# A graph network on one core: count products packed per group of eight nodes through three PSUM banks, and one PSUM bank for the attention sums

## The chip, the cores and the metric

The kernel runs on one core of a Trainium2 chip. Its time is the device time of one execution in microseconds (us), launch to end, as the median of several executions. A profiled execution gives one trace with the start and duration of each instruction on each engine: TensorE (PE, with its weight loads PEld), VectorE (DVE), ScalarE (ACT), GpSimd (POOL), SyncE (SP), whose queue (SPq) issues DMAs.

## What is computed

A graph of 6,250 nodes with 256 features and 100,000 edges sorted by destination. Two residual blocks:

```python
edge_index = jnp.stack([src, dst])
h = jnp.maximum(_layernorm(x, axis=-1), 0.0)
x = x + attention(h, edge_attr_16, edge_attr_4, W_n, attn_l, attn_r, attn_m, src, dst)
h = jnp.maximum(_layernorm(x, axis=-1), 0.0)
x = x + three_sage_layers(h, edge_index, ...)

# attention: 8 heads of 32 columns
e = leaky_relu((left[src] + right[dst] + edge part) / 3)    # per edge and head
a = softmax of e over the edges of one destination
out[dst] = sum over its edges of a * (feat @ W_n)[src]

# one SAGE layer
msg  = relu(x @ pW + pb)[src]
mean = segment_sum(msg, dst) / max(degree, 1)
out  = mean @ lW + lb + x @ rW, divided by its norm
```

## The kernel before, in words

Nodes are held in 49 blocks of 128, edges in 784 tiles of 128; seven tiles make a chunk, so there are 112 chunks. The kernel has three stages: preparation (projections into a table of rows), attention over the chunks, and the three SAGE layers. The change lies in the attention stage.

**The attention loop.** Every engine runs its own loop over steps `c` with the chunks taken at fixed offsets, in an order written out by hand; semaphores tie the engines. `Count.done(n)` is the value that the n-th signal of a semaphore makes, `free(n)` the value that says a buffer is free again; the number beside a name in `ATTENDED` is how many buffers are free at the start.

- GpSimd gathers the 896 source rows of a chunk with seven indirect DMAs into a ring of `RING = 7` chunks (`gather_chunk`, L621). The gather of chunk c waits for `summed(c - 7)`.
- TensorE, step c: a front part for the scores (`kinds_of`, `kind_tiles`, `to_heads`, `to_edges`, `left_of`; L1824 to L1862), then the sums of chunk c-1 (`sum_tiles`): for each of seven tiles a product of a one-hot matrix with the weighed rows (L1874, 128x265, float32, so two instructions each), accumulated in one PSUM bank, and one more product that adds what the chunk before left in the same window of nodes, moved by `shift_mat` (L1882). Its end is the signal `summed(c - 1)`. After it, in some steps, the projection of a finished block of nodes (`project`, L1930) or its transposition (`turn`, L1892).
- VectorE, step c: `below_max(c-1)` (L1999), `score_of(c+2)`, `run_maxima(c)` (ends with L1991), `weigh(c-1)` (L2014, the long product of rows and weights), the marks (below), then pieces of the work for a finished block of nodes (`biased`, `node_norm`, `node`) in 7 of 16 steps each, and `shifting(c)`.
- ScalarE, step c: `soften(c-1)` (L2166, L2167), `own_side(c)` (the one-hot matrices of the sums: seven times L2187, then L2191), `keep(c-2)` (L2197: sums from PSUM to SBUF), `other_side(c+4)` (L2175, L2178), and `turned`, `normed`, `positive` for a block of nodes.
- SyncE loads the edges of later chunks and stores the sums that `keep` has copied.

**The counts.** Beside the attention, in the 96 steps from 8 to 103, the stage builds a dense matrix of edge counts for the first 3,072 nodes, which the layers read later. Its 384 groups of eight nodes (`WIN = 8`) are taken in pairs, 192 duos, two duos to a step. For a duo q: VectorE writes marks (`mark`, eight compares, L2085 and L2086) into one of `MARKS = 3` buffers; TensorE forms the counts (`cross`, L1921: two accumulated float16 products for each of the two groups, 128x392 each, into banks 3 and 4); ScalarE packs both banks into bytes in one instruction (`pack`, L2221, 128x784). After 16 groups a stripe of 128 columns is complete and a DMA on ScalarE's queue stores it. `cross(q)` waits for `packed(q - 1)`, since there is one pair of banks.

**The order around the counts.** TensorE, step c: front part, `cross` of the first duo, four tiles of the sums (`HELD = 4`), `cross` of the second duo, three tiles and the shift. ScalarE, step c: `soften(c-1)`, `pack` of the first duo of step c-1, `own_side(c)`, `pack` of the second duo of step c-1, `keep(c-2)`, `turned`, `other_side(c+4)`, `normed`, `positive`. `own_side(c)` waits for `summed(c - 2)`, because it overwrites the one-hot matrices that those sums read. The sums of even and odd chunks lie in PSUM banks 6 and 7. In PSUM, bank 0 holds the scores, 1 the transposed scores, 2 the weights, 5 the block of nodes.

Of the kernel before, what the change touches and what calls it, by code (L numbers as in the profile page):

```python
# [35 lines left out]
ACT = mybir.ActivationFunctionType  # L36
# [7 lines left out]
TILES = 7  # L44
CHUNK = TILES * P
CHUNKS = -(-E // CHUNK)
# [1 line left out]
RING = 7  # L48
EDGES = 6
ENDS = 2  # L50
HELD = 4
assert CHUNKS % SLOTS == 0
TABLE = BLOCKS * P + P
FALL = 128
# [37 lines left out]
WIN = 8  # L92
WINS = DENSE // WIN
CROSS = BLOCKS * WIN
# [9 lines left out]
STRIPE = P  # L104
# [3 lines left out]
MARKS = 3  # L108
# [522 lines left out]
    return list(range(DUOS * (c - CROSS_FROM) // steps, DUOS * (c + 1 - CROSS_FROM) // steps))  # L631


def first_duo(c):

    return duos_at(c)[:1]


def later_duos(c):

    return duos_at(c)[1:]


def buffer_of(stripe):
# [569 lines left out]
def layers(nc, m, a, block, s, stored):  # L1214
# [461 lines left out]
ATTENDED = dict(  # L1676
    rows0=None, rows1=None, rows2=None, rows3=None, rows4=None, rows5=None, rows6=None, ends0=None, ends1=None, edges0=None,
    edges1=None, edges2=None, edges3=None, edges4=None, edges5=None, distance=0, oht=0, right=1, kinds=1, masked=0,
    scored=0, leaky=0, xt=1, bwd=0, mt=1, diff=1, expd=2, denoms=0, weighed=0, apart=0, onehot=0, shifted=0, summed=2, kept=2,
    store0=None, store1=None, sums=None, recips=0, norm=0, x1=0, stats=0, mv=0, newton=0, inv_norm=0, shift=0,  # L1680
    h=0, x1_put=None, htrans=0, ht=0, proj=0, evac=0, relu=0, put=None, runs=None, sorting=0, picked=0, taken=0, marked=0, crossed=0, packed=0, built0=None, built1=None)

# [1 line left out]
def attention(nc, m, a, block, s):  # L1684
# [132 lines left out]
    def _(pe):  # L1817
# [46 lines left out]
        def sum_tiles(c, tiles):  # L1864
            if not 0 <= c < CHUNKS:
                return
            parity, k = c % 2, c % RING
            if tiles[0] == 0:
                pe.wait_ge(s["denoms"].sem, s["denoms"].done(c))
                pe.wait_ge(s["weighed"].sem, s["weighed"].done(c))  # L1870
                pe.wait_ge(s["onehot"].sem, s["onehot"].done(c))
                pe.wait_ge(s["kept"].sem, s["kept"].free(c))
            for t in tiles:
                last = nc.tensor.matmul(m.ps[:, 6 + parity, 0:SUMC], m.one_hot[:, parity, t, :], m.ring[:, k, t, 0:SUMC],  # L1874
                                        start=(t == 0), stop=(c == 0 and t == TILES - 1))
            if tiles[-1] < TILES - 1:
                return
            if c:

                pe.wait_ge(s["kept"].sem, s["kept"].done(c - 1))  # L1880
                pe.wait_ge(s["shifted"].sem, s["shifted"].done(c - 1))
                last = nc.tensor.matmul(m.ps[:, 6 + parity, 0:SUMC], m.shift_mat[:, parity, :], m.sums_out[:, 1 - parity, :],  # L1882
                                        start=False, stop=True)
            last.then_inc(s["summed"].sem, 1)

# [22 lines left out]
                                        start=(j == 0), stop=(j == SORTS - 1))  # L1908
            last.then_inc(s["picked"].sem, 1)

        def cross(q):


            pe.wait_ge(s["marked"].sem, s["marked"].done(q))
            if q:
                pe.wait_ge(s["packed"].sem, s["packed"].done(q - 1))
            else:
                pe.wait_ge(s["taken"].sem, s["taken"].done(3))
            for i in range(2):
                for r in range(2):  # L1920
                    last = nc.tensor.matmul(m.ps[:, 3 + i, 0:CROSS], m.lane_marks[:, q % MARKS, 2 * i + r, :], m.cell_marks[:, q % MARKS, 2 * i + r, :],  # L1921
                                            start=(r == 0), stop=(r == 1))
            last.then_inc(s["crossed"].sem, 1)

        def project(n):
# [8 lines left out]
        for c in range(-4, steps):  # L1934
            if 0 <= c + 3 < CHUNKS:
                kinds_of(c + 3)
            kind_tiles(c + 3, range(0, TILES))
            if 0 <= c + 1 < CHUNKS:
                to_heads(c + 1)
            if 0 <= c < CHUNKS:  # L1940
                to_edges(c)
            if 0 <= c + 3 < CHUNKS:
                left_of(c + 3)
            for q in first_duo(c):
                cross(q)
            sum_tiles(c - 1, range(0, HELD))
            for q in later_duos(c):
                cross(q)
            sum_tiles(c - 1, range(HELD, TILES))
            if SORT_FROM < c <= SORT_FROM + 4:  # L1950
                pick(c - SORT_FROM - 1)
            for n in at_step(c, 3):
                project(n)
            for n in at_step(c, 2):
                turn(n)

    @block.vector
    def _(dve):
# [118 lines left out]
        def mark(q):  # L2077


            if q >= MARKS:  # L2080
                dve.wait_ge(s["crossed"].sem, s["crossed"].done(q - MARKS))
            for i in range(2):
                for r in range(2):
                    w = 2 * q + i
                    nc.vector.tensor_scalar(m.cell_marks[:, q % MARKS, 2 * i + r, :], m.cell_row, m.cell_at[:, r, w:w + 1], None, ALU.is_equal)  # L2085
                    last = nc.vector.tensor_scalar(m.lane_marks[:, q % MARKS, 2 * i + r, :], m.cell_row[:, 0:P], m.lane_of[:, r, w:w + 1],  # L2086
                                                   None, ALU.is_equal)
            last.then_inc(s["marked"].sem, 1)

        def node(n):  # L2090

# [68 lines left out]
    def _(act):  # L2160
# [32 lines left out]
        def keep(c):  # L2193
            act.wait_ge(s["summed"].sem, s["summed"].done(c))
            if c >= 2:
                act.wait_ge(s[f"store{c % 2}"], 16 * (c // 2))
            nc.scalar.activation(m.sums_out[:, c % 2, :], m.ps[:, 6 + c % 2, 0:SUMC], ACT.Copy).then_inc(s["kept"].sem, 1)  # L2197

        def normed(n):
            act.wait_ge(s["shift"].sem, s["shift"].done(n))  # L2200
# [8 lines left out]
                act.wait_ge(s["proj"].sem, s["proj"].done(n - 1))  # L2209
            nc.scalar.activation(m.b_hT[:], m.turned_h, ACT.Copy).then_inc(s["ht"].sem, 1)  # L2210

        def pack(q):


            stripe, place = divmod(q, STRIPE_DUOS)
            buffer = buffer_of(stripe)
            act.wait_ge(s["crossed"].sem, s["crossed"].done(q))
            if place == 0 and stores_before(stripe, buffer):
                act.wait_ge(s[f"built{buffer}"], 16 * stores_before(stripe, buffer))
            out = m.stripes[:, buffer, :].rearrange("p (b n) -> p b n", n=STRIPE)[:, :, 2 * WIN * place:2 * WIN * (place + 1)]  # L2220
            nc.scalar.activation(out.rearrange("p b (i n) -> p i b n", i=2), m.ps[:, 3:5, 0:CROSS].rearrange("p i (b n) -> p i b n", n=WIN),  # L2221
                                 ACT.Copy).then_inc(s["packed"].sem, 1)
            if place == STRIPE_DUOS - 1:
                act.wait_ge(s["packed"].sem, s["packed"].done(q))
                act.dma_start(m.adj[stripe], m.stripes[:, buffer, :]).then_inc(s[f"built{buffer}"], 16)

        def positive(n):
# [3 lines left out]
        for c in range(-4, steps):  # L2231
            if 0 <= c - 1 < CHUNKS:
                soften(c - 1)
            for q in first_duo(c - 1):
                pack(q)
            if 0 <= c < CHUNKS:
                own_side(c)
            for q in later_duos(c - 1):
                pack(q)
            if 0 <= c - 2 < CHUNKS:  # L2240
                keep(c - 2)
            for n in at_step(c, 3):
                turned(n)
            if 0 <= c + 4 < CHUNKS:
                other_side(c + 4)
            for n in at_step(c, 1):
                normed(n)
            for n in at_step(c, 4):
                positive(n)
# [454 lines left out]
```

## Time and profile before

| | |
|---|---|
| time, median of 3 executions | 3049.98 us (3046.11 to 3052.17) |
| the profiled execution | 3053.74 us, its span 3052.0 us |
| mean granted TensorE clock in it | 0.943 |
| busy over the span: PE / PEld / DVE / ACT / POOL | 87% / 61% / 73% / 54% / 66% |
| DMA | mean 207 GB/s |

The span is what the profiler covers of one execution, from the first instruction to the last; 1.7 us lie around it. Busy shares are means over stages with different limits, so each stage has to be read by itself. "Idle before" an instruction is time in which its engine did nothing, put down to what released it last.

### The profile page before, as it was taken

What the parts mean: (1) busy time and instruction counts of PE and PEld (TensorE: products, weight loads), DVE (VectorE), ACT (ScalarE), POOL (GpSimd) and SP (SyncE); (2) the same over time, 40 slices, a digit from 0 to 9 for tenths busy, and PEclk for the clock granted to TensorE, in tenths of its full rate; (3) what the DMA queues carried; (4) which work ended last, traced back from release to release, by engine and by line L of the source; (5) the groups of instructions that cost most, each with busy time, mean ns of one, the idle gap of its engine ahead of it and who ended that gap; (6) DMA issues with size and microseconds to landing.
All of it is one profiled execution on the core that took longest, in us unless ns stands there. A gap on an engine that the chain in (4) does not pass through costs nothing.

```text
span 3052.0 us, 48723 instructions
## 1 busy us (share of the span) xinstructions
PE 2645.6 (87%) x13426; PEld 1861.6 (61%) x13426; DVE 2223.2 (73%) x7629; ACT 1652.6 (54%) x3538; POOL 2005.0 (66%) x2041
## 2 busy tenths in 40 slices
PE   7698888888888888979999998899999988988894
PEld 5466666666666666746666664566666655655562
DVE  6369899899898988845666665566666656878885
ACT  5347776777677666635554553455555533444430
POOL 3576666666666666357776665777766757777772
PEclk9689999999999999979999999999999998999996
DMA  8766777777777776567776763777766557777762
GB/s 236 214 189 197 211 216 215 216 211 211 217 217 212 216 199 199 158 209 217 222 222 207 216 196 118 238 227 222 216 206 191 176 179 227 244 238 240 240 207 71
DMA packets 455091, 630.35 MB, mean 207 GB/s; under 512 B 94496, under 2 KB 373088, under 8 KB 454816
## 3 DMA queue, kind: packets, MB, share of 16 engines
q0 software_dynamic: 97184, 280.55, 33.0%
q1 hardware_dynamic: 325568, 301.63, 31.7%
q10 hardware_dynamic: 32064, 44.98, 4.0%
q8 instruction: 116, 1.90, 0.3%
q14 instruction: 159, 1.30, 0.1%
HBM read 551.28 MB, written 75.63 MB: 205 GB/s over the span
## 4 chain that ended last, share of the span: by engine, by line
PE 50%; ACT 19%; issue 10%; DVE 9%; POOL 5%; DMA 2%; ACTq 0%; SPq 0%; DVEq 0%; POOLq 0%
PE ps L1297 21%; ACT one_hot L2187 7%; PE ps L1874 7%; PE ps L1349 5%; PE ps L1371 4%; ACT root L2221 4%; PE ps L1335 4%; POOL ring L1242 3%; PE ps L1921 3%; PE ps L1309 3%; ACT attention_work L2175 3%; PE ps L1882 2%; POOL ring L621 2%; DVE block_cube L798 1%; PE ps L692 1%
## 5 line engine op out<-in xcount | busy, mean ns | idle before, releaser
L1242 POOL DMA_INDIRECT ring<-message_table,src_index x1209 | 1183.1, 979 | 559.9 <-issue 379.4
L621 POOL DMA_INDIRECT ring<-attention_table,src_index x784 | 795.6, 1015 | 367.6 <-issue 211.0
L1297 PE MATMUL ps<-count_rows,high_rows 128*128 128x512 f32 x1764 | 759.5, 431 | 98.4 <-ACT attention_work L1629 71.5
L1297 PE MATMUL ps<-count_rows,low_rows 128*128 128x512 f32 x1764 | 719.9, 408 | 0.0
L1639 ACT ACTIVATE count_rows<-one_hot 128x512 fp32r<-128x512 uint8 x882 | 524.7, 624 | 185.7 <-PE ps L1297 174.1
L1297 PEld LDWEIGHTS ps<-count_rows,high_rows 128*128 128x128 f32 x1764 | 347.3, 197 | 214.2 <-issue 91.6
L2187 ACT ACTIVATE one_hot<-iota_row,dst_rel 128x128 f32<-128x128 f32 x784 | 241.2, 388 | 307.6 <-PE ps L1882 303.6
L1518 DVE CAST high_rows<-attention_work 128x512 fp32r<-128x512 f32 x441 | 192.7, 437 | 293.9 <-PE ps L1297 276.7
L1874 PE MATMUL ps<-ring,one_hot 128*128 128x265 f32 x1568 | 404.3, 402 | 1.8 <-issue 1.7
L1297 PEld LDWEIGHTS ps<-count_rows,low_rows 128*128 128x128 f32 x1764 | 347.3, 197 | 74.8
L1874 PEld LDWEIGHTS ps<-ring,one_hot 128*128 128x128 f32 x1568 | 308.6, 200 | 61.8 <-issue 5.1
L1520 DVE TENSOR_TENSOR low_rows<-attention_work,high_rows 128x512 fp32r<-128x512 f32 x441 | 309.2, 701 | 15.2
L1921 PE MATMUL ps<-cell_marks,lane_marks 128*128 128x392 f16 x768 | 165.5, 339 | 137.7 <-ACT root L2221 136.8
L2014 DVE TENSOR_TENSOR ring<-ring,ps 128x1792 f32<-128x1792 f32 x112 | 224.4, 2003 | 30.2 <-ACT ps L2166 29.6
L2085 DVE TENSOR_SCALAR cell_marks<-cell_row,cell_at 128x392 f16<-128x392 f16 x768 | 243.2, 317 | 0.0
L1371 PE MATMUL ps<-ring,attention_work 128*32 128x256 f32 x2418 | 199.3, 401 | 17.6 <-DMA ring<-message_table,src_index 16.3
L1335 PE MATMUL ps<-w_l,attention_work 128*128 128x256 f32 x588 | 163.2, 402 | 52.7 <-DVE attention_work L1451 30.6
L1833 PEld LDWEIGHTS ps<-attention_work 128*128 128x128 f32 x1568 | 199.7, 198 | 13.2 <-ACT attention_work L2178 12.8
L1921 PEld LDWEIGHTS ps<-cell_marks,lane_marks 128*128 128x128 f16 x768 | 66.2, 98 | 223.3 <-issue 189.9
L1833 PE MATMUL ps<-attention_work 128*128 128x32 f32 x1568 | 191.5, 275 | 11.6 <-ACT attention_work L2178 11.6
L1349 PE MATMUL ps<-w_pr,block_hT 128*128 128x512 f32 (+1 forms) x400 | 191.7, 604 | 0.9 <-ACT block_hT L1569 0.9
L2086 DVE TENSOR_SCALAR lane_marks<-cell_row,lane_of 128x128 f16<-128x128 f16 x768 | 189.4, 247 | 0.0
(199 smaller groups left out, 3699.0 us busy)
## 6 DMA issues: line engine op xcount, KB each, us to landing
attention_work<-message_table SPq DMA_DIRECT2D x432, 256.0 KB
one_hot<-dense_adjacency SPq DMA_DIRECT2D x126, 448.0 KB, 4.2
attention_work<-in_dst_edges SPq DMA_DIRECT2D x112, 448.0 KB
ring<-message_table,src_index POOLq DMA_INDIRECT x1209
dense_adjacency<-root ACTq DMA_DIRECT2D x24, 784.0 KB, 4.4
attention_sums<-sums_out SPq DMA_DIRECT2D x112, 132.5 KB, 2.5
ring<-attention_table,src_index POOLq DMA_INDIRECT x784
message_table<-attention_work ACTq DMA_DIRECT2D x98, 128.0 KB, 3.2
```

The lines of the kernel that those rows point to most:

```text
L621: pool.indirect_dma_start(m.ring[:, k, t, 0:cols], None, table, bass.IndirectOffsetOnAxis(ap=m.src[:, at:at + 1], axis=0)).then_inc(s[f"ro ...
L1242: pool.indirect_dma_start(m.quad_ring[:, k, j, :], None, m.tables[w.l], bass.IndirectOffsetOnAxis(ap=m.src[:, t:t + 1], axis=0)).then_inc( ...
L1297: last = nc.tensor.matmul(m.ps[:, 2 + half, 0:cols], rows[:, v % SPLITS, half * P:(half + 1) * P], m.a_rows[:, k, 0:cols], start=(j == 0 a ...
L1335: last = nc.tensor.matmul(m.ps[:, 0, 0:D], sides[k], m.w_l[:, w.l, k, :], start=(k == 0), stop=(k == 1))
L1349: last = nc.tensor.matmul(to, m.b_hT[:, k * P:(k + 1) * P], m.w_pr[:, w.l + 1, k, cols], start=(k == 0), stop=(k == 1))
L1371: last = nc.tensor.matmul(m.ps[j * LANE:(j + 1) * LANE, 6 + u % 2, 0:D], m.lane_hot[:, u % 2, j * DEPTH + r, :], m.quad_ring[:, v % QUADS, ...
L1520: nc.vector.tensor_tensor(low, rows, high.bitcast(fp32), ALU.subtract).then_inc(s["split"].sem, 1)
L1639: nc.scalar.activation(m.a_rows[:, u % STREAM, 0:cols].rearrange("p (k n) -> p k n", n=STRIPE), m.a_small[:, g % BUNCHES, 0:cols // STRIPE ...
L1833: last = nc.tensor.matmul(m.ps[:, 0, t * 32:(t + 1) * 32], m.one_hotT[:, t * P:(t + 1) * P], m.right[:, c % EDGES, :], start=False, stop=F ...
L1874: last = nc.tensor.matmul(m.ps[:, 6 + parity, 0:SUMC], m.one_hot[:, parity, t, :], m.ring[:, k, t, 0:SUMC], start=(t == 0), stop=(c == 0 a ...
L1921: last = nc.tensor.matmul(m.ps[:, 3 + i, 0:CROSS], m.lane_marks[:, q % MARKS, 2 * i + r, :], m.cell_marks[:, q % MARKS, 2 * i + r, :], sta ...
L2187: last = nc.scalar.activation(m.one_hot[:, c % 2, t, :], m.iota_row[:, 0:P], ACT.Abs, bias=m.dst_rel[:, at:at + 1], scale=-1.0)
```

## The change

- The counts are handled by single groups g instead of duos. `cross(g)` writes one bank out of the ring 3, 4, 7 and waits for `packed(g - 3)`; `pack(g)` is one ScalarE instruction over one bank (128x392). There are 384 of each. The products and the marks stay as many as they were; `mark` signals after each group.
- TensorE, step c: a `cross` of one group ahead of tiles 0 and 1, of tiles 2 and 3, of tiles 4 and 5, and of tile 6 with the shift.
- ScalarE, step c: `soften(c-1)`, `pack` of groups 1, 2 and 3 of step c-1, `keep(c-2)`, `own_side(c)`, `pack` of group 0 of step c, `turned`, `other_side(c+4)`, `normed`, `positive`.
- All chunks' sums lie in bank 6, and `kept` has one buffer, so the first tile of a chunk waits for the `keep` of the chunk before.

```diff
-HELD = 4
+CROSS_BANKS = [3, 4, 7]
...
-def first_duo(c):
-    return duos_at(c)[:1]
-def later_duos(c):
-    return duos_at(c)[1:]
+def groups_at(c):
+    return [2 * q + i for q in duos_at(c) for i in range(2)]
+def group_at(c, place):
+    return groups_at(c)[place:place + 1]
+def cross_bank(g):
+    return CROSS_BANKS[g % len(CROSS_BANKS)]
...
-    scored=0, leaky=0, xt=1, bwd=0, mt=1, diff=1, expd=2, denoms=0, weighed=0, apart=0, onehot=0, shifted=0, summed=2, kept=2,
+    scored=0, leaky=0, xt=1, bwd=0, mt=1, diff=1, expd=2, denoms=0, weighed=0, apart=0, onehot=0, shifted=0, summed=2, kept=1,
...
+            sums = m.ps[:, 6, 0:SUMC]
...
-                last = nc.tensor.matmul(m.ps[:, 6 + parity, 0:SUMC], m.one_hot[:, parity, t, :], m.ring[:, k, t, 0:SUMC],
+                last = nc.tensor.matmul(sums, m.one_hot[:, parity, t, :], m.ring[:, k, t, 0:SUMC],
...
-        def cross(q):
-            pe.wait_ge(s["marked"].sem, s["marked"].done(q))
-            if q:
-                pe.wait_ge(s["packed"].sem, s["packed"].done(q - 1))
+        def cross(g):
+            pe.wait_ge(s["marked"].sem, s["marked"].done(g))
+            if g >= len(CROSS_BANKS):
+                pe.wait_ge(s["packed"].sem, s["packed"].done(g - len(CROSS_BANKS)))
             else:
                 pe.wait_ge(s["taken"].sem, s["taken"].done(3))
-            for i in range(2):
-                for r in range(2):
-                    last = nc.tensor.matmul(m.ps[:, 3 + i, 0:CROSS], m.lane_marks[:, q % MARKS, 2 * i + r, :], m.cell_marks[:, q % MARKS, 2 * i + r, :],
-                                            start=(r == 0), stop=(r == 1))
+            for r in range(2):
+                mark = 2 * (g % 2) + r
+                last = nc.tensor.matmul(m.ps[:, cross_bank(g), 0:CROSS], m.lane_marks[:, g // 2 % MARKS, mark, :],
+                                        m.cell_marks[:, g // 2 % MARKS, mark, :], start=(r == 0), stop=(r == 1))
...
-            for q in first_duo(c):
-                cross(q)
-            sum_tiles(c - 1, range(0, HELD))
-            for q in later_duos(c):
-                cross(q)
-            sum_tiles(c - 1, range(HELD, TILES))
+            for place, tiles in enumerate(((0, 1), (2, 3), (4, 5), (6,))):
+                for g in group_at(c, place):
+                    cross(g)
+                sum_tiles(c - 1, tiles)
...
-                dve.wait_ge(s["crossed"].sem, s["crossed"].done(q - MARKS))
+                dve.wait_ge(s["crossed"].sem, s["crossed"].done(2 * (q - MARKS) + 1))
...
-            last.then_inc(s["marked"].sem, 1)
+                last.then_inc(s["marked"].sem, 1)
...
-            nc.scalar.activation(m.sums_out[:, c % 2, :], m.ps[:, 6 + c % 2, 0:SUMC], ACT.Copy).then_inc(s["kept"].sem, 1)
+            nc.scalar.activation(m.sums_out[:, c % 2, :], m.ps[:, 6, 0:SUMC], ACT.Copy).then_inc(s["kept"].sem, 1)
...
+            out = m.stripes[:, buffer, :].rearrange("p (b n) -> p b n", n=STRIPE)[:, :, WIN * place:WIN * (place + 1)]
+            nc.scalar.activation(out, m.ps[:, cross_bank(g), 0:CROSS].rearrange("p (b n) -> p b n", n=WIN),
                                  ACT.Copy).then_inc(s["packed"].sem, 1)
...
-            for q in first_duo(c - 1):
-                pack(q)
+            for g in groups_at(c - 1)[1:]:
+                pack(g)
+            if 0 <= c - 2 < CHUNKS:
+                keep(c - 2)
             if 0 <= c < CHUNKS:
                 own_side(c)
-            for q in later_duos(c - 1):
-                pack(q)
-            if 0 <= c - 2 < CHUNKS:
-                keep(c - 2)
+            for g in group_at(c, 0):
+                pack(g)
```

## Rows read from the trace of the kernel before

**Rows 1.** Stretches: us; busy PE, PEld, DVE, ACT, POOL (instructions); clock, DMA share, GB/s.

```profile
226.00:1236.00 1010.00, 873.18 (x4649) 659.41 (x4649) 906.11 (x3312) 712.29 (x1559) 680.03 (x667) 0.98 0.73 210
1236.00:1294.00 58.00, 55.14 (x271) 43.16 (x269) 47.59 (x142) 41.31 (x106) 18.38 (x20) 1.00 0.51 149
```

**Rows 2.** Waits from 226 to 1236 us: us in total, times, longest us.

```profile
ACT one_hot L2187 <- PE ps L1882: 277.5, 96, 4.5
...
POOL ring L621 <- PE ps L1882: 156.6, 92, 6.4
PE ps L1921 <- ACT root L2221: 136.8, 141, 3.5
DVE ring L2014 <- ACT ps L2166: 26.9, 39, 1.5
...
DVE attention_work L1999 <- PE ps L1862: 18.5, 14, 1.5
DVE attention_work L1968 <- PE ps L1841: 13.3, 31, 0.4
...
DVE block_msg L2126 <- PE ps L1930: 5.9, 26, 0.6
```

**Rows 3.** Groups by line, 226 to 1236 us: busy us, mean ns, idle before.

```profile
L2014 DVE TENSOR_TENSOR ring<-ring,ps 128x1792 f32<-128x1792 f32 x96 | 192.4, 2004 | 27.5 <-ACT ps L2166 26.9
...
L621 POOL DMA_INDIRECT ring<-attention_table,src_index x667 | 680.4, 1020 | 332.0 <-issue 175.4 <-PE ps L1882 156.6
```

**Rows 4.** ScalarE in order of time over one step: start us, us, instruction.

```profile
607.06 2.15 ACT L2187 ACTIVATE one_hot<-iota_row,dst_rel 128x128 f32<-128x128 f32 x7 [2.79 <-PE ps L1882]
...
610.10 0.81 ACT L2221 ACTIVATE root<-ps 128x784 uint8<-128x784 f32 x1
610.81 0.39 ACT L2197 ACTIVATE sums_out<-ps 128x265 f32<-128x265 f32 x1
611.08 1.04 ACT L2175 ACTIVATE attention_work<-attention_work,window_p 128x896 f32<-128x896 int32 x1
...
613.01 0.58 ACT L2203 ACTIVATE block_h<-block_o,block_shift,block_inv_norm 128x256 f32<-128x256 f32 x1
...
614.08 0.80 ACT L2221 ACTIVATE root<-ps 128x784 uint8<-128x784 f32 x1
```

**Rows 5.** TensorE in order of time, the second duo of the same step.

```profile
615.03 0.82 PE L1921 MATMUL ps<-cell_marks,lane_marks 128*128 128x392 f16 x4 [0.88 <-ACT root L2221]
615.69 1.50 PE L1874 MATMUL ps<-ring,one_hot 128*128 128x265 f32 x6
```

**Rows 6.** VectorE in order of time over one step.

```profile
612.49 0.20 DVE L1999 TENSOR_TENSOR attention_work<-attention_work,ps 128x56 f32<-128x56 f32 x1
...
614.77 1.99 DVE L2014 TENSOR_TENSOR ring<-ring,ps 128x1792 f32<-128x1792 f32 x1
616.68 0.31 DVE L2085 TENSOR_SCALAR cell_marks<-cell_row,cell_at 128x392 f16<-128x392 f16 x1
...
619.83 0.14 DVE L2094 TENSOR_SCALAR block_degree<-block_sums 128x1 f32<-128x1 f32 x1
```

**Rows 7.** TensorE in order of time in a step without counts.

```profile
1248.93 0.55 PE L1824 MATMUL ps<-attn_edge,attention_work 112*128 112x224 f32 x2
...
1251.89 3.29 PE L1874 MATMUL ps<-ring,one_hot 128*128 128x265 f32 x14
...
1255.47 1.88 PE L1930 MATMUL ps<-w_pr,block_hT 128*128 128x512 f32 x4
1257.18 0.54 PE L1824 MATMUL ps<-attn_edge,attention_work 112*128 112x224 f32 x2
```

**Rows 8.** TensorE in order of time after the stage's longest wait.

```profile
1110.21 1.26 PE L1921 MATMUL ps<-cell_marks,lane_marks 128*128 128x392 f16 x4 [3.48 <-ACT root L2221]
1111.26 2.79 PE L1874 MATMUL ps<-ring,one_hot 128*128 128x265 f32 x6
```

**Rows 9.** GpSimd in order of time, one gather of a tile.

```profile
617.91 1.21 POOL L621 DMA_INDIRECT ring<-attention_table,src_index  x1 [2.15 <-PE ps L1882]
```

More of the change, by code:

```diff
@@ L1881, in sum_tiles @@
                 pe.wait_ge(s["shifted"].sem, s["shifted"].done(c - 1))
-                last = nc.tensor.matmul(m.ps[:, 6 + parity, 0:SUMC], m.shift_mat[:, parity, :], m.sums_out[:, 1 - parity, :],
+                last = nc.tensor.matmul(sums, m.shift_mat[:, parity, :], m.sums_out[:, 1 - parity, :],
                                         start=False, stop=True)
@@ L2210, in turned, with pack @@
             nc.scalar.activation(m.b_hT[:], m.turned_h, ACT.Copy).then_inc(s["ht"].sem, 1)
-        def pack(q):
-            stripe, place = divmod(q, STRIPE_DUOS)
+        def pack(g):
+            stripe, place = divmod(g, 2 * STRIPE_DUOS)
             buffer = buffer_of(stripe)
-            act.wait_ge(s["crossed"].sem, s["crossed"].done(q))
+            act.wait_ge(s["crossed"].sem, s["crossed"].done(g))
             if place == 0 and stores_before(stripe, buffer):
                 act.wait_ge(s[f"built{buffer}"], 16 * stores_before(stripe, buffer))
-            out = m.stripes[:, buffer, :].rearrange("p (b n) -> p b n", n=STRIPE)[:, :, 2 * WIN * place:2 * WIN * (place + 1)]
-            nc.scalar.activation(out.rearrange("p b (i n) -> p i b n", i=2), m.ps[:, 3:5, 0:CROSS].rearrange("p i (b n) -> p i b n", n=WIN),
+            out = m.stripes[:, buffer, :].rearrange("p (b n) -> p b n", n=STRIPE)[:, :, WIN * place:WIN * (place + 1)]
+            nc.scalar.activation(out, m.ps[:, cross_bank(g), 0:CROSS].rearrange("p (b n) -> p b n", n=WIN),
                                  ACT.Copy).then_inc(s["packed"].sem, 1)
-            if place == STRIPE_DUOS - 1:
-                act.wait_ge(s["packed"].sem, s["packed"].done(q))
+            if place == 2 * STRIPE_DUOS - 1:
+                act.wait_ge(s["packed"].sem, s["packed"].done(g))
                 act.dma_start(m.adj[stripe], m.stripes[:, buffer, :]).then_inc(s[f"built{buffer}"], 16)
```

## The prediction, made before the changed kernel was run

> **What bounds the kernel now.** I first asked where the change can act at all: the counts are made between 226 and 1236 us, so I cut the span into stretches. That one is 1010 us long and VectorE is busy for 906.11 of it, TensorE for 873.18, ScalarE for 712.29, GpSimd for 680.03 [rows 1]. The reader is to see that no engine is full, and that two are close. The groups by line give 96 of the long products, one to a step, so a step takes 1010 / 96 = 10.52 us [rows 3]; just behind the stretch, where no counts are made, TensorE alone is nearly full (55.14 of 58) and a step of it is much shorter [rows 1, 7].
>
> Second, the waits of that stretch, to see who holds whom [rows 2]. TensorE loses 136.8 us, 1.42 us a step, at the count products, waiting for ScalarE's packing. ScalarE loses 277.5 us, once in each of the 96 steps, at the one-hot matrices, waiting for the end of the sums. Each of the two waits for the other: that is a loop, not a full engine. GpSimd loses 156.6 us behind the same end of the sums. VectorE loses 26.9 + 18.5 + 13.3 + 5.9 = 64.6 us in small pieces.
>
> Third, the loop itself, in order of time. ScalarE starts `own_side` at 607.06, packs one duo at 610.10, keeps the sums at 610.81, makes the other side from 611.08 to 613.01, then the block's work and `soften`, and packs the next duo at 614.08 [rows 4]. TensorE stood idle for it for 0.88 us, starts the second duo's products at 615.03 and the last three tiles at 615.69 [rows 5]; those tiles and the shift (four products of 0.45, worked out below) end about 617.5, and only then may ScalarE start the next `own_side`. Around the loop: 7.02 us on ScalarE, 0.95 to hand over, 0.66 for the count products and 1.8 for the rest of the sums, 10.4 us. That is the 10.52 us step. So one bank pair for the counts, packed once ahead of and once behind `own_side`, sets the pace.
>
> **The change part by part.** A look at each engine without its waits gives the floors that are left when the loop is cut.
>
> TensorE: 873.18 / 96 = 9.10 us a step [rows 1]. The count products stay 768 in number. A duo costs 615.69 - 615.03 = 0.66 us from start to start [rows 5], a group 0.33; splitting moves them and adds no instruction. The new waits (`packed` of three groups back, `kept` of the chunk before) are costed as places in the order below.
>
> ScalarE: a pack of 784 columns costs 0.71 us from its start to the next, the keep of 265 columns 0.27 [rows 4]. That is 0.85 ns a column, and gives 0.38 us for 392 columns. Four cost 1.52 us against 1.42 for two: 0.1 us a step more. Bounds: nothing more (each exactly half of 0.71), or each still 0.71, which would be 1.42 us a step more. I take 0.1, since the row of 265 columns is near to 392. ScalarE's step without waits is then 712.29 / 96 + 0.1 = 7.5 us, at the upper bound 8.8. Either is covered by VectorE's floor, so it costs nothing; without that cover it would cost up to the same 0.1 to 1.4 us a step. The stripe stores stay 24 DMAs on ScalarE's queue and are issued one `own_side` earlier.
>
> GpSimd: seven gathers a chunk of 1020 ns with some 0.3 us of issue each make 9.2 us a step [rows 3, 9]; it waits 1.63 us of each step now, for `summed`. It has no order changed.
>
> VectorE: the marks keep their 16 instructions a step, one signal more for each duo, taken as nothing (bounds: nothing, or twice what VectorE idles outside its named waits for each instruction, (1010 - 906.11 - 64.6) / 3312 = 0.012 us: 0.02 us a step, 2 us in all). Its step without the named waits is (1010 - 64.6) / 96 = 9.85 us [rows 1, 2]. It is the highest floor.
>
> Now the new order, to see whether VectorE would still wait. Let D be the start of L1999 in a step. From its rows, the weighing starts at D + 2.3, the marks at D + 4.2 and end at D + 7.3 [rows 6]; 16 marks in 3.15 us make four groups, ready at D + 5.0, 5.8, 6.6 and 7.3. TensorE needs 1251.89 - 1248.93 = 2.96 us for the front part, 1255.47 - 1251.89 = 3.58 for seven tiles and the shift (eight products of 0.45), 1257.18 - 1255.47 = 1.71 for a projection in 7 of 16 steps [rows 7]. With the first group at D + 5.0, it ends the sums at D + 5.0 + 4 x 0.33 + 3.58 = D + 9.9, the projection at D + 11.6, the next front part at D + 12.9 or D + 14.6. The next first group is marked at D + 9.85 + 5.0 = D + 14.85. So TensorE is there first, by 0.2 to 2 us, and now waits for VectorE instead of ScalarE. VectorE needs from that front part only the one of the step before, done by D + 4.8 at the latest for its start at D + 9.85.
>
> ScalarE: the first group's products end at D + 5.4, its pack at about D + 6.0 (0.24 to hand over, as between the end of a pack and the start of products now), the other side at D + 8.0, `normed` (behind VectorE's statistics, which are its last work of the step) at D + 10.4, `soften` right after; the weighing that needs it starts at D + 12.15. Then three packs to D + 12, `keep` 0.27 after the end of the sums, `own_side` 3.04, to about D + 15.3, and the next first pack is due at D + 15.4. No wait on VectorE arises from this.
>
> The two waits that are added on TensorE: the first tile needs the `keep` of the chunk before. Behind it is queued all the rest of TensorE's step, and for that wait VectorE's marks, `own_side` and the gathers. It is due at D' + 5.4 (D' the next start) and there at D' + 2.5. The fourth group needs the pack of the first group of the same step, which stands behind `keep` and `own_side`: due at D + 5.0 + 3 x (0.33 + 0.90) = D + 8.7, there at D + 6.0. The loop from `summed` over keep, `own_side`, pack, fourth group and the last two products is 0.27 + 3.04 + 0.38 + 0.24 + 0.33 + 0.90 = 5.2 us, half of what it was.
>
> So the step should fall from 10.52 to about 9.85 us: 64.6 us over 96 steps if every named wait of VectorE goes. I leave 6 us for waits of the first steps and of the last four stripes, which share one buffer: 59 us. The sum is made against the profiled 3053.74, which becomes 2995; the median shown is 3.8 us below it, so 2991. The layers behind, and the 16 steps without counts, keep their times: there `keep` also comes ahead of `own_side`, and TensorE's front part of 2.96 us covers it.
>
> TensorE's clock: behind the stage's longest wait, 3.48 us, the same six instructions took 2.79 us instead of 1.50 [rows 5, 8]; the granted clock over the stretch was 0.98 [rows 1], so waits of about 1 us leave it at its upper level of 2.4 GHz. The Trainium skill, "TensorE: Matmul & The Clock Gate", section "A second HAM failure mode: psum-queue depth-cycling", speaks against this change: it reports a kernel that cycled through PSUM banks in each iteration, idled briefly between its groups of products, and whose clock kept falling and rising. The stretch of before, with two waits a step, does not show it. By the row the clock costs nothing here; by that rule the slower rival below.
>
> **The rivals.** *The loop is only moved.* If ScalarE comes to `keep` and `own_side` over 2.7 us later than I wrote, because it stands in line for the third and fourth group's products, TensorE waits at the fourth group and a step takes perhaps 10.3. Against: ScalarE's floor of 7.5. Then (10.52 - 10.3) x 96 = 21 us are saved: 3029.
>
> *GpSimd becomes the bound, nothing is gained.* While VectorE makes marks a gather took 1.21 us [rows 9] against the mean of 1.02 [rows 3]. If VectorE's fuller step made all gathers that long, seven of 1.21 + 0.3 would be 10.57 us: the step of now, 3050. Against: VectorE's instructions don't change, only 0.7 us of its idle time goes.
>
> *The clock falls: slower.* TensorE's idle time gathers at one place, ahead of the first group, up to 2 us. At full clock its work is 873.18 x 0.98 = 856 us. Under a mean granted clock of 856 / 1010 = 0.85 it is longer than the stretch is now, and from there on it decides. At 0.83 the stretch is 1031 us: 21 more, 3071. For: the row behind the 3.48 us wait. Against: the waits of now, 136.8 us in 141, so 0.97 us each [rows 2], at a clock of 0.98.
>
> **How the numbers follow.** My forecast 0.70 (2975 to 3008: 2975 if 10 of VectorE's remaining 39 us of idle time go too, 3008 if 0.2 us a step stay as waits), the moved loop 0.13, more gained than 75 us 0.04, no gain 0.05, slower 0.08. Faster by over 0.2% (6 us, about what this measurement can tell): 0.70 + 0.13 + 0.04 = 0.87; within it 0.05; slower 0.08. The range leaves out the two last and the one below: 2975 to 3030.
>
> **What would show it.** Right: TensorE's wait for the packing (136.8 us) nearly gone, and one of some 0.7 us a step for VectorE's marks in its place; VectorE over 95% busy between the same steps; its named waits under 10 us; ScalarE's wait ahead of the one-hot matrices now at `keep` or at the packs; pack at about 0.5 us each; a step of 9.8 to 9.9; clock 0.95 or more. Wrong: `PE L1921` still waiting for ScalarE's packing, tiles of the sums waiting for `keep`, gathers of mean 1.1 us or more with TensorE waiting for rows, or a granted clock under 0.9.

## The result, and the profile after

The changed kernel takes 2972.55 us (median of 5, 2969.79 to 2974.6) against 3049.98: 0.975 of the time, interval 0.9739 to 0.9761. On a second occasion, beside the kernel before, it took 2969.73 against 3049.46, 0.9743 (0.9725 to 0.9761). Forecast were 2991 in a range of 2975 to 3030. The direction and the mechanism came as written; the gain is 77 to 80 us instead of 59, and the time lies 2.5 us below the range.

Three stretches of the two traces follow. Their edges are starts of VectorE's first instruction of a step (L1999, L2004 in the changed kernel): the 96 steps from step 9 to step 104 (all but the last make counts; step 8, the first with counts, lies ahead), the seven steps 105 to 111, and the rest with the layers. Columns: us; busy PE, PEld, DVE, ACT, POOL; clock, DMA share, GB/s. The kernel before:

```profile
225.90:1236.50 1010.60, 873.78 (x4652) 659.65 (x4651) 906.21 (x3313) 712.86 (x1560) 680.36 (x667) 0.98 0.73 210
1236.50:1286.80 50.30, 47.89 (x242) 38.41 (x243) 41.45 (x122) 38.61 (x99) 18.04 (x19) 1.00 0.54 157
1286.80:3052.00 1765.20, 1547.66 (x7791) 1032.40 (x7789) 1152.17 (x3820) 793.13 (x1629) 1183.11 (x1209) 0.93 0.66 205
```

The changed kernel:

```profile
226.20:1163.60 937.40, 875.67 (x4653) 663.52 (x4654) 902.98 (x3313) 739.79 (x1756) 666.42 (x671) 0.97 0.78 228
1163.60:1210.80 47.20, 45.06 (x222) 35.64 (x221) 41.09 (x122) 33.88 (x90) 15.14 (x16) 0.96 0.52 147
1210.80:2970.70 1759.90, 1543.94 (x7797) 1029.07 (x7796) 1154.48 (x3820) 794.12 (x1632) 1181.57 (x1209) 0.94 0.67 205
```

A step takes 937.4 / 96 = 9.76 us instead of 1010.6 / 96 = 10.53. VectorE does the same 3313 instructions and is now busy for 96% of the stretch instead of 90%; TensorE follows with 93% (875.67 of 937.4). Who waits there now, in the changed kernel (us in total, times, longest us):

```profile
POOL ring L621 <- PE ps L1889: 83.1, 46, 4.4
ACT block_h L2208 <- DVE block_shift L2124: 75.8, 40, 2.7
PEld ps L1928 <- DVE lane_marks L2091: 67.6, 62, 1.8
ACT ps L2171 <- DVE attention_work L2004: 41.8, 40, 1.5
ACT root L2226 <- PE ps L1928: 41.3, 75, 1.3
...
PE ps L1928 <- DVE lane_marks L2091: 32.1, 35, 1.4
...
ACT root L2226 <- DMA dense_adjacency<-root: 13.2, 4, 4.5
PE ps L1830 <- DVE attention_work L1973: 12.9, 13, 1.3
PE ps L1928 <- ACT one_hot L2196: 12.7, 12, 1.3
...
PE ps L1928 <- ACT root L2226: 3.3, 2, 1.9
...
DVE ring L2019 <- ACT ps L2171: 1.0, 2, 0.8
```

Beside [rows 2] the reader is to see three things. TensorE's 136.8 us behind the packing have become 3.3; it waits 32.1 us for marks instead (its weight loads, which are listed apart and overlap the products, 67.6). ScalarE no longer waits 277.5 us for the sums, but for VectorE (`normed` 75.8, `soften` 41.8). And VectorE, which everybody waits for, waits for nobody: 1.0 us instead of 68.6 (the 64.6 of the prediction and one row of 4.0 that it left out).

ScalarE in order of time over one step of the changed kernel, to be read beside [rows 4]:

```profile
599.70 0.39 ACT L2202 ACTIVATE sums_out<-ps 128x265 f32<-128x265 f32 x1 [0.40 <-PE ps L1889]
599.99 2.14 ACT L2192 ACTIVATE one_hot<-iota_row,dst_rel 128x128 f32<-128x128 f32 x7
602.16 0.95 ACT L2196 ACTIVATE one_hot<-one_hot 128x896 f32<-128x896 f32 x1
603.21 0.50 ACT L2226 ACTIVATE root<-ps 128x392 uint8<-128x392 f32 x1
...
603.87 1.04 ACT L2180 ACTIVATE attention_work<-attention_work,window_p 128x896 f32<-128x896 int32 x1
...
606.93 0.60 ACT L2208 ACTIVATE block_h<-block_o,block_shift,block_inv_norm 128x256 f32<-128x256 f32 x1 [1.04 <-DVE block_shift L2124]
...
607.72 1.25 ACT L2226 ACTIVATE root<-ps 128x392 uint8<-128x392 f32 x3
```

The sums are kept first, the one-hot matrices follow at once, and only one pack stands between them and the other side. Three packs follow each other in 1.25 us: (1.25 - 0.49) / 2 = 0.38 us from one to the next, the price taken.

### The profile page after: what moved, and what is told of

Read it like the earlier page. It is cut to its first block, busy times and chain, and to the rows that moved or that the text cites. A ratio compares the mean times of both kernels' runs of the same rounds, so it can differ in the third digit from the quotient of the medians.

```text
span 2970.7 us, 49107 instructions
## 1 busy us (share of the span) xinstructions
PE 2640.5 (89%) x13426; PEld 1859.5 (63%) x13426; DVE 2221.8 (75%) x7629; ACT 1676.1 (56%) x3730; POOL 1985.5 (67%) x2041
## 3 DMA queue, kind: packets, MB, share of 16 engines
q0 software_dynamic: 97184, 280.55, 33.4%
## 4 chain that ended last, share of the span: by engine, by line
PE 43%; DVE 36%; issue 7%; POOL 6%; ACT 3%; DMA 2%; DVEq 0%; SPq 0%; POOLq 0%; ACTq 0%
PE ps L1303 21%; DVE cell_marks L2090 6%; DVE ring L2019 6%; PE ps L1355 5%; PE ps L1377 4%; DVE lane_marks L2091 4%; POOL ring L1248 4%; PE ps L1341 4%; PE ps L1315 3%; DVE block_cube L804 2%; POOL ring L621 2%; PE ps L1881 2%; DVE block_ey L1993 2%; DVE block_inv_norm L806 2%; DVE attention_work L1996 2%
## 5 line engine op out<-in xcount | busy, mean ns | idle before, releaser
L621 POOL DMA_INDIRECT ring<-attention_table,src_index x784 | 777.7, 992 | 308.0 <-issue 225.0
L1881 PE MATMUL ps<-ring,one_hot 128*128 128x265 f32 x1568 | 438.6, 404 | 2.2 <-issue 2.1
L1881 PEld LDWEIGHTS ps<-ring,one_hot 128*128 128x128 f32 x1568 | 304.7, 201 | 63.5 <-issue 8.2
L2090 DVE TENSOR_SCALAR cell_marks<-cell_row,cell_at 128x392 f16<-128x392 f16 x768 | 254.6, 332 | 0.0
L1928 PE MATMUL ps<-cell_marks,lane_marks 128*128 128x392 f16 x768 | 198.5, 341 | 48.9 <-DVE lane_marks L2091 32.5
L2019 DVE TENSOR_TENSOR ring<-ring,ps 128x1792 f32<-128x1792 f32 x112 | 222.6, 1988 | 3.2 <-ACT ps L2171 3.2
L2226 ACT ACTIVATE root<-ps 128x392 uint8<-128x392 f32 x384 | 169.6, 488 | 61.8 <-PE ps L1928 46.7
L1839 PE MATMUL ps<-attention_work 128*128 128x32 f32 x1568 | 191.6, 276 | 13.3 <-ACT attention_work L2183 13.2
```

Of the source, the lines that this page charges most:

```text
L621: pool.indirect_dma_start(m.ring[:, k, t, 0:cols], None, table, bass.IndirectOffsetOnAxis(ap=m.src[:, at:at + 1], axis=0)).then_inc(s[f"ro ...
L1839: last = nc.tensor.matmul(m.ps[:, 0, t * 32:(t + 1) * 32], m.one_hotT[:, t * P:(t + 1) * P], m.right[:, c % EDGES, :], start=False, stop=F ...
L1881: last = nc.tensor.matmul(sums, m.one_hot[:, parity, t, :], m.ring[:, k, t, 0:SUMC], start=(t == 0), stop=(c == 0 and t == TILES - 1))
L2019: nc.vector.tensor_tensor(ring_heads[k][:, :, :, 0:HD], ring_heads[k][:, :, :, 0:HD], weights[:, :, :, None].to_broadcast([P, TILES, HEADS ...
```

## The experiments

Each kernel was timed beside the kernel before on the same chip. Two of the four groups of runs fell on two chips on which every kernel, the one before too, took 440 to 670 us longer (the one before 3582.95 and 3594.58 us instead of 3050). They were repeated on two other chips, and the conclusions rest on the repeats; what the slow chips showed stands at the end.

**ScalarE's order alone.** The kernel before, with duos, one pair of banks, two banks of sums and TensorE's old order:

```diff
-            for q in first_duo(c - 1):
-                pack(q)
-            if 0 <= c < CHUNKS:
-                own_side(c)
             for q in later_duos(c - 1):
                 pack(q)
             if 0 <= c - 2 < CHUNKS:
                 keep(c - 2)
+            if 0 <= c < CHUNKS:
+                own_side(c)
+            for q in first_duo(c):
+                pack(q)
```

> The kernel before with ScalarE's order alone: the second duo's pack and keep ahead of the one-hot matrices, the first duo's pack of the same step behind them. Duos, one pair of banks, four and three tiles, two banks of sums stay. If a loop ScalarE-TensorE set the step and VectorE is the floor under it: the loop is 0.27 + 3.04 + 0.71 + 0.24 + 0.66 + 1.8 = 6.7 us, so VectorE's waits go as in the changed kernel and the time is 2970 to 2985. Rival, that the ring of three banks and the spreading carry the gain: TensorE still waits at each duo for the pack of the one before, 3020 or more.

> The kernel before with ScalarE's order alone, once more, since on the first chip every kernel, the one before too, was about 530 us longer, with idle times of 2 to 5 us on each engine in turn. By the loop theory, where the kernel before takes its 3050: 2970 to 2985, with VectorE's named waits under 10 us. By the rival (the ring and the spreading carry the gain): 3020 or more, with TensorE still waiting over 80 us for packs.

Measured: 2979.87 us, 0.9763 (0.9739 to 0.9787). The 96 steps, then the seven behind them:

```profile
226.60:1165.60 939.00, 877.11 (x4656) 673.16 (x4655) 901.89 (x3314) 724.77 (x1564) 670.64 (x670) 0.96 0.79 227
1165.60:1212.80 47.20, 44.79 (x229) 35.70 (x228) 41.06 (x123) 35.28 (x94) 16.01 (x17) 1.00 0.55 158
```

Its waits:

```profile
PE ps L1921 <- DVE lane_marks L2086: 51.9, 41, 2.3
...
PE ps L1921 <- ACT root L2221: 6.0, 4, 1.9
DVE ring L2014 <- ACT ps L2166: 3.5, 7, 1.4
```

939.0 us for the stretch against 937.4 of the whole change: the reordered queue of one engine brings the gain without the ring, the single groups or the spreading. VectorE's named waits are down to 3.5 us here. The loop theory's 2970 to 2985 held, the rival's 3020 fell. 7 us lie between the medians of this kernel and of the changed one, but the two intervals of the ratio overlap; they were not separated.

**The ring with nearly the old order.** The changed kernel, with this on ScalarE:

```diff
-            for g in groups_at(c - 1)[1:]:
+            for g in groups_at(c - 1)[:2]:
                 pack(g)
-            if 0 <= c - 2 < CHUNKS:
-                keep(c - 2)
             if 0 <= c < CHUNKS:
                 own_side(c)
-            for g in group_at(c, 0):
+            for g in groups_at(c - 1)[2:]:
                 pack(g)
+            if 0 <= c - 2 < CHUNKS:
+                keep(c - 2)
```

> The changed kernel with ScalarE's order nearly as before: two packs ahead of the one-hot matrices, two packs and keep behind them. The fourth group's products wait for the pack of the first group, which comes after the other side and soften of the next step: 3.04 + 0.76 + 0.27 + 1.93 + 1.07 + 0.38 + 0.24 + 0.33 + 0.9 = 8.9 us, and keep stands behind 3.04 + 0.76 us of other work, so the first tile waits about 1 us for it. By the loop theory both lie under VectorE's 9.77 us, but close in steps with a projection: 2975 to 3000. Rival, that the order is what counts: 3030 or more.

> The changed kernel with ScalarE's order nearly as before, once more. By the loop theory 2975 to 3000: the loops of 8.9 us that are left lie under VectorE's 9.77, but not in each step. By the rival (the order is what counts): 3030 or more.

Measured: 2988.44 us, 0.9778 (0.9756 to 0.98). The same two stretches:

```profile
229.70:1165.00 935.30, 863.39 (x4646) 655.12 (x4646) 896.03 (x3313) 730.20 (x1753) 673.64 (x669) 0.98 0.79 227
1165.00:1220.80 55.80, 49.84 (x227) 38.85 (x227) 41.79 (x123) 34.50 (x88) 16.76 (x18) 0.91 0.51 139
```

Its TensorE waits for `keep`, in the 96 steps and then from 1165 to 1236 us:

```profile
PE ps L1881 <- ACT sums_out L2202: 55.7, 54, 1.5
```

```profile
PE ps L1881 <- ACT sums_out L2202: 10.2, 6, 3.2
```

Where counts are made this is as fast as the change (935.3), although the first tile waits 55.7 us for `keep`, the 1 us a time that was expected: that wait lies under VectorE's floor. So either of the two edits, ScalarE's order alone or the rest of the change with nearly the old order, cuts the loop, and their gains don't add. (The rest is the ring, the single groups and TensorE's spread order together; no run took them apart.) What is lost against the change is lost outside: 8.6 us in the seven steps (55.8 against 47.2), where the same wait is no longer covered, and up to 12 in all that follows (2992.7 - 1220.8 = 1771.9 against 1759.9, with a few us of chance in it). Step 9 starts anywhere from 224.7 to 230.2 us in these traces, so its 3.5 us more say little.

**One bank for the sums.** The kernel before with `m.ps[:, 6, 0:SUMC]` for both parities in the tile products, the shift product and `keep`, and:

```diff
...
-    ... shifted=0, summed=2, kept=2,
+    ... shifted=0, summed=2, kept=1,
...
```

> The kernel before with all sums in bank 6 and one free buffer of kept, nothing else. Keep is done 3.04 + 0.71 + 0.27 + 0.1 = 4.1 us after the sums, the first tile is due 2.96 + 0.66 = 3.6 us after them: TensorE waits 0.5 us there, but the second duo waits for ScalarE anyway (0.9 us), so the time is as before, 3044 to 3056. Rival: the wait adds up, 0.5 x 112 = 56 us more.

> The kernel before with one bank of sums, once more. 3044 to 3056, since the wait of 0.5 us for keep is taken out of the second duo's wait of 0.9 us. Rival: up to 56 us more. On the first chip it was 0.7% slower, at the edge of its interval, which would be 21 us here.

Measured: 3063.95 us, 1.0036 (1.0023 to 1.0049), so 7 to 15 us slower, where 3044 to 3056 was expected. The 96 steps and the seven behind them:

```profile
230.20:1238.60 1008.40, 873.93 (x4651) 657.52 (x4652) 906.48 (x3314) 712.92 (x1560) 668.00 (x667) 0.98 0.74 210
1238.60:1294.60 56.00, 49.02 (x229) 38.11 (x229) 41.83 (x121) 35.71 (x90) 18.02 (x19) 0.94 0.50 142
```

With counts the wait is hidden as reckoned (1008.4). The reckoning forgot the 16 steps without them, where TensorE is nearly full [rows 1]. TensorE and ScalarE in such a step:

```profile
1258.19 3.37 PE L1874 MATMUL ps<-ring,one_hot 128*128 128x265 f32 x14 [0.42 <-ACT sums_out L2197]
```

```profile
1254.63 2.15 ACT L2187 ACTIVATE one_hot<-iota_row,dst_rel 128x128 f32<-128x128 f32 x7 [1.95 <-PE ps L1882]
...
1257.67 0.38 ACT L2197 ACTIVATE sums_out<-ps 128x265 f32<-128x265 f32 x1
```

`keep` stands 3.04 us of one-hot matrices behind the end of the sums, TensorE's front part lasts 2.96. Six such waits make 10.1 us behind 1238.6. In the changed kernel the one bank costs nothing that can be seen: its seven steps take 47.2 us, as do those of the order alone with two banks. There `keep` stands ahead of `own_side`.

**Less work on VectorE: a faster kernel.** The changed kernel with the shift matrix made by ScalarE, behind the other side:

```diff
...
-            nc.vector.tensor_scalar(m.shift_mat[:, c % 2, :], m.step[:], m.shift_by[:, c:c + 1], None,
-                                    ALU.is_equal).then_inc(s["shifted"].sem, 1)
...
+            nc.scalar.activation(m.shift_mat[:, c % 2, :], m.step[:], ACT.Abs, bias=m.shift_by[:, c:c + 1],
+                                 scale=-1.0).then_inc(s["moved"].sem, 1)
+            act.wait_ge(s["moved"].sem, s["moved"].done(c - 1))
+            nc.scalar.activation(m.shift_mat[:, c % 2, :], m.shift_mat[:, c % 2, :], ACT.Relu, bias=1.0,
+                                 scale=-1.0).then_inc(s["shifted"].sem, 1)
...
```

> The changed kernel with the shift matrix of each chunk made on ScalarE (Abs and Relu, two instructions of 128x128 behind the other side) instead of VectorE (one instruction of 0.32 us, 0.19 to 0.24 from start to start). If VectorE is the floor and ScalarE's 2 us of idle time a step are free: 0.2 x 111 = 22 us less, 0.32 x 111 = 36 at most, so 2937 to 2955. Rival, that ScalarE or the loop sets the step now: no gain, or up to 0.6 us a step lost, 2972 to 3030.

> The changed kernel with the shift matrix made on ScalarE, once more. If VectorE is the floor: 2937 to 2955. If ScalarE or TensorE sets the step by now: 2965 or more.

Measured: 2955.17 us, 0.9675 (0.9654 to 0.9696), the fastest kernel of the study and at the upper edge of the 2937 to 2955 expected. The 96 steps:

```profile
228.20:1145.60 917.40, 872.39 (x4653) 664.16 (x4653) 878.83 (x3218) 789.55 (x1946) 673.61 (x669) 0.97 0.80 232
```

VectorE is busy for 24.2 us less (902.98 - 878.83), and the stretch is 20.0 us shorter. ScalarE took 50 us of work for it. The 4.2 us between the two are VectorE's named waits, which rose from 1.0 to 5.2.

**More work on either engine.** One more 128x128 compare a chunk on VectorE into a spare tile, in the changed kernel and in the kernel before; and, in the changed kernel, one more 128x512 pass on ScalarE:

```diff
+            nc.vector.tensor_scalar(m.spare[:], m.step[:], m.shift_by[:, c:c + 1], None, ALU.is_equal)
             nc.vector.tensor_scalar(m.shift_mat[:, c % 2, :], m.step[:], m.shift_by[:, c:c + 1], None,
```

```diff
+            nc.scalar.activation(m.spare[:], m.dst_bc[:, c % ENDS, 0:512], ACT.Abs, bias=m.window_p[:, c:c + 1], scale=-1.0)
             nc.scalar.activation(m.one_hotT, m.dst_bc[:, c % ENDS, :], ACT.Abs, bias=m.window_p[:, c:c + 1],
```

> The changed kernel with one more VectorE instruction in each chunk: the 128x128 compare of the shift matrix once more, into a spare tile, 0.19 to 0.32 us. If VectorE is the floor, nearly all of it comes through: 111 x 0.19 to 0.32 = 21 to 36 us more than the changed kernel. If something else sets the step: under 6 us.

> The changed kernel with one more ScalarE instruction in each chunk, 128x512 into a spare tile, about 0.6 us, ahead of the other side's first pass: 0.6 x 112 = 67 us of work. ScalarE idles 2 us a step, so if it only follows VectorE, 0 to 8 us more. If its order is tight (the rival): 30 us or more.

> The kernel before with the same one more VectorE instruction. There VectorE idles 0.7 us a step at named waits and the ScalarE-TensorE loop sets the step, so most is absorbed: 0 to 10 us more. If VectorE were the bound there too: 21 to 36.

> The changed kernel once more, beside the kernel before on the same chip: 0.9739 to 0.9761 of it. Its profile shows how much the layers behind the attention vary by themselves: if the 5.3 us that they were shorter in the first profile are chance, they come out anywhere within 5 us of either.

The four fell on one of the slow chips and were repeated:

> The changed kernel with one more VectorE instruction of 0.19 to 0.32 us in each chunk, once more, where the kernel before takes its 3050. VectorE the floor: 21 to 36 us more than the changed kernel, so 2992 to 3010. Something else: 2972 to 2980.

> The changed kernel with one more ScalarE instruction of about 0.6 us in each chunk, once more. ScalarE only follows VectorE: 2970 to 2982. Its order is tight: 3000 or more.

> The kernel before with one more VectorE instruction in each chunk, once more. Absorbed by the 0.7 us a step that VectorE waits: 3048 to 3060. VectorE the bound there too: 3070 to 3086.

> The changed kernel once more: ratio 0.9739 to 0.9761, 2970 to 2976. If the 3 us in the last eight steps and the 5 us in the layers are chance, its profile has them within 5 us of the kernel before; the 73 us between steps 8 and 104 come out within 2 us again.

| kernel | median us | ratio to the kernel before | steps 9 to 104, us | VectorE busy there, us |
|---|---|---|---|---|
| changed, once more | 2969.73 | 0.9743 (0.9725 to 0.9761) | 935.8 | 901.6 |
| changed, more VectorE | 2985.87 | 0.979 (0.9772 to 0.9808) | 950.0 | 915.0 |
| changed, more ScalarE | 2974.41 | 0.9752 (0.9727 to 0.9776) | 939.9 | 905.2 |
| before, more VectorE | 3048.47 | 0.9997 (0.9987 to 1.0006) | 1008.1 | 921.5 |

The windows view of the first (the 96 steps and the seven behind), of the second (the 96) and of the fourth (both):

```profile
227.80:1163.60 935.80, 877.74 (x4657) 666.16 (x4656) 901.57 (x3313) 737.81 (x1756) 671.53 (x670) 0.97 0.78 228
1163.60:1210.80 47.20, 45.07 (x222) 35.70 (x221) 41.13 (x122) 33.91 (x90) 15.65 (x17) 0.96 0.54 154
```

```profile
227.70:1177.70 950.00, 885.13 (x4657) 668.94 (x4656) 914.96 (x3409) 740.60 (x1756) 674.66 (x671) 0.96 0.77 225
```

```profile
225.80:1233.90 1008.10, 870.52 (x4652) 657.62 (x4651) 921.50 (x3409) 712.75 (x1560) 674.33 (x667) 0.98 0.73 210
1233.90:1284.80 50.90, 48.73 (x239) 38.85 (x239) 42.52 (x128) 37.33 (x96) 18.04 (x19) 0.97 0.52 155
```

In the changed kernel 13.4 us more of VectorE's busy time made the stretch 14.2 us longer; in the kernel before 15.3 us more were absorbed whole, and VectorE's named waits fell from 68.6 to 51.4. That is the floor shown from both sides. The median rose by 16 us, which lies between the ranges written for the two readings (2972 to 2980, 2992 to 3010); the stretch decides between them. The 21 us or more of the first reading were too many: an instruction whose row says 0.28 us added 0.14 us to the sum, part of its row overlapping its neighbours'. ScalarE's 0.71 us a chunk, 68 us over the stretch, cost 4.1 us of it, under the 8 allowed for an engine that only follows.

## Why the prediction was right in kind and wrong in size

**The loop.** Right. Predicted was a loop ScalarE to TensorE of 10.4 us, its end when packs and keep no longer surround `own_side`, and VectorE as the next bound. TensorE's wait for the packing went from 136.8 to 3.3 us, the order alone does the same, and work added to VectorE counts in the one kernel and not in the other.

**The step that failed: "64.6 us over 96 steps if every named wait of VectorE goes. I leave 6 us".** That term, 59 us, was mis-sized: 67.6 us of named waits went. It was also the whole sum, and the other 14 us that the two traces differ by were put at nothing. In VectorE's own accounts over the 96 steps:

| term | forecast | measured |
|---|---|---|
| VectorE's named waits, before to after | 64.6 to 6: -58.6 | 68.6 to 1.0: -67.6 |
| its idle time outside them | 0 | 35.8 to 33.4: -2.4 |
| its busy time, same 3313 instructions | 0 (2 more at most) | 906.2 to 903.0: -3.2 |
| the seven steps behind | 0 | 50.3 to 47.2: -3.1 |
| the rest, mostly the layers | 0 | 1765.2 to 1759.9: -5.3 |
| sum | -59 | -81.6 |

(The traces also differ by 0.3 us ahead of step 9; the medians by 77.4.) 9 of the 22.6 us between are the waits: one row of 4.0 left out of the sum, and an allowance for leftovers that the written-out order gave no reason for; by that order VectorE waits for nobody, and so it was. The four single-buffered stripes, for which part of it was meant, did hold ScalarE for 13.2 us at the stores, and TensorE behind it for the 3.3 us of its two waits for packs, but no row of VectorE waits for that. In the kernel before it was otherwise: the row of 4.0 is one wait for a projection, at 1116.3 us, behind the TensorE wait of 3.48 us of [rows 8], and that one stood behind a pack which a stripe's store had held up for 1.90 us. The range's lower end, 2975, took all 64.6 us and 10 of VectorE's remaining idle time; without the few us of the layers below, the median would lie inside it. (The inner bound 3008 does not come out of its own terms, 0.2 us a step on the forecast: 2991 + 0.2 x 96 is 3010, without the 6 us it is 3005. Nothing hangs on it.)

**"The 16 steps without counts keep their times."** Right, although the seven steps seem 3.1 us shorter. Their edges lie on VectorE, and the new order has shifted TensorE against it: between these edges TensorE does 222 products in the changed kernel and 242 in the one before. From TensorE's end of the sums in step 104 to that in step 112 it does its 249 or 250 in both. The kernel before, its run with more VectorE, the changed kernel and the order alone:

```profile
1240.60:1293.40 52.80, 50.29 (x250) 39.35 (x248) 44.76 (x131) 36.70 (x98) 15.00 (x16) 1.00 0.47 133
1238.10:1292.80 54.70, 51.99 (x249) 40.35 (x247) 45.81 (x138) 36.48 (x99) 14.92 (x16) 0.97 0.45 130
1164.70:1219.20 54.50, 51.99 (x249) 40.42 (x247) 45.83 (x137) 36.06 (x98) 14.35 (x15) 0.97 0.45 129
1166.60:1219.40 52.80, 50.29 (x250) 39.34 (x248) 45.77 (x136) 35.97 (x95) 15.32 (x16) 1.00 0.49 142
```

In either order the eight steps take 52.8 us at a granted clock of 1.00 and 54.5 to 54.7 at 0.97. By the same edges one bank in the old order takes 60.6 us (clock 0.97) and the ring with nearly the old order 63.5 (0.92), so what that pairing costs there is real. The 96 steps are hardly moved by the choice of edges: 1010.4 to 938.6 us on TensorE, 71.8 less, against 73.2 on VectorE.

**The layers.** From TensorE's end of the sums in step 112 to the end, the four traces with `keep` behind `own_side` (the kernel before, more VectorE in it, one bank, the ring) have 1754.9 to 1759.6 us, the six with `keep` ahead of it 1747.4 to 1754.4. No instruction of the layers was changed. The two sets don't overlap and their means lie 5.6 us apart, so chance alone is an unlikely reading, but the nearest two traces differ by 0.5 us and nothing here shows a cause. (The granted clock is 0.93 in two of the four and 0.94 in the other eight; those of the four at 0.94 have 1754.9 and 1756.8.) It stays open, and with it some 5 us of the gain.

**TensorE, places.** Forecast was a wait for marks of some 0.7 us a step, 67 in all. The weight loads of the count products wait 67.6 us for marks, the products themselves 32.1. The 12.7 us put down to `own_side` (L2196) are more of the same: all twelve stand at the first group of a step, which needs nothing that follows `own_side` on ScalarE, and in each of them the products start 0.06 us after the end of their last mark, as in the rows put down to the marks. `own_side` only happened to end 0.02 to 0.04 us before that start. 12.9 us are for the scores; all together it idles 61.7 us, 0.64 a step. The added wait for `keep` is in no row of the stretch. At the fourth group, where the prediction feared one, there are two waits in 96 steps, the 3.3 us behind stripe stores.

**ScalarE.** Price of a pack 0.38, as taken. Its wait moved to `normed` and `soften`, not to the packs alone (41.3 us): it arrives ahead of VectorE.

**GpSimd.** Gathers were not slower (busy 666.4 us in the stretch against 680.4; the repeats have 671.5 and, in the kernel before with more VectorE, 674.3), so the second rival had no ground. Its wait for ring space fell from 156.6 to 83.1 us.

**The clock.** 0.97 over the stretch after 0.98, and 0.95 to 0.97 in the other kernels with the loop cut by ScalarE's order. TensorE's idle time hardly brought it down, and the slower rival fell with it: the failure that the Trainium skill reports for cycled banks ("TensorE: Matmul & The Clock Gate", "A second HAM failure mode: psum-queue depth-cycling") is not seen here, with waits of at most 1.9 us at the count products.

**The moved loop.** It was given 0.13 and did not come. It would have needed `own_side` 2.7 us late; `own_side` starts 0.3 us after `keep`, which waited 0.40 us for the sums.

## What to carry to other kernels

When two engines each wait for the other once in every step and neither is full, write out the loop between them and look for work that merely stands inside it in the queue: taking it out of one engine's order brought 72 us here, as much as three buffers with a spread order did. The gain ends at the next fullest engine, so sum its waits, all of its rows, and take off only what a place in the new order leaves; then move work off it. And look at an edit in the steps where its cover is missing: in the old order one bank less was free in 96 steps and cost 7 to 15 us in the others. Last, a reordering shifts the engines against each other, so a short stretch between edges on one engine can gain or lose another engine's work: count the instructions between the edges before reading the time.

## What the runs showed of the hardware

- A VectorE row is not its price, and the price depends on the neighbours. Compares of 128x128 with a row of 0.28 us, put beside one like it, added 0.14 and 0.16 us each to the busy time (13.4 us for 96 where VectorE was full, 15.3 where it wasn't). The one compare taken off VectorE in the faster kernel gave back 0.25 us each (24.2 for 96).
- The same kernels on two other chips. There the kernel before took 3582.95 and 3594.58 us. VectorE's and ScalarE's instructions were not slower (the long product took 1986 ns in the median in the changed kernel and 1988 there), but engines often stood still for 2 us and more. Many of these waits have no releaser that the profile can name (`remote`); at ScalarE's packs they sum to 182.2 us in the changed kernel, the longest 10.7 us:

```profile
ACT root L2226 <- remote: 182.2, 82, 10.7
```

- The kernels ranked differently there. The changed kernel was at 0.9476 (0.9406 to 0.9545), the ring with nearly the old order at 0.9776 (0.9713 to 0.9839), the order alone at 1.011 (1.0003 to 1.0217), one bank at 1.0073 (1.0034 to 1.0113), the shift on ScalarE at 0.9616 (0.9547 to 0.9685); the changed kernel with more VectorE 0.9557 (0.9491 to 0.9623), with more ScalarE 0.9589 (0.9522 to 0.9655), the one before with more VectorE 1.0037 (0.9993 to 1.0082). There the whole change was worth 5%, the ring with nearly the old order 2% and the bare order nothing. That slack between engines is what pays where stalls fall on any of them is one reading, but it is not shown: no run took it apart, the groups ran on different chips, and what stops the engines there stays open.
